# Which queue issues a perceiver kernel's last transfers: from SyncE's queue to ScalarE's, and the last two steps moved one by one

## The reference, cut to what matters

```
x = x + xattn(layernorm(x), ctx)      # 16 heads of 64: softmax(q k^T / 8) v, then @ w_out + b_out
x = x + attn(layernorm(x))            # three mixes of x with x shifted by one token,
                                      # k, v, r = their products; a decaying running sum over 512 tokens; @ Wo + bo
x = x + relu(layernorm(x) @ w1 + b1) @ w2 + b2
```

## Time and profile before

| | |
|---|---|
| three runs | 2408.26, 2411.14, 2415.79 us; median 2411.14 |
| the profiled execution | 2409.01 us, its span 2407.2 us |
| PE busy | 2300.2 us, 96% |
| DVE busy | 1833.4 us, 76% |
| ACT busy | 1545.8 us, 64% |
| POOL busy | 1606.9 us, 67% |
| DMA | 438.94 MB, mean 182 GB/s |

### The profile page before, as it was taken

The page is one execution under the profiler, slowest core; times in us unless marked ns, Lnnn a source line. Parts: engine busy times, 40 slices in busy tenths (PEclk is TensorE's granted clock), DMA queues, the critical chain, the costliest instruction groups (busy, mean ns, idle before and its releaser), DMA issues.

```text
span 2407.2 us, 44073 instructions
## 1 busy us (share of the span) xinstructions
PE 2300.2 (96%) x13696; PEld 2103.8 (87%) x13696; DVE 1833.4 (76%) x3669; ACT 1545.8 (64%) x2690; POOL 1606.9 (67%) x799
## 2 busy tenths in 40 slices
PE   4968999999999999999999999999999998879999
PEld 3648989999999999999999999999999998768788
DVE  7766777777777777777777777777777777679884
ACT  4655666667666676667666766767666765555444
POOL 2006878888888888888888888888888885421111
PEclk9989999999999999999999999999999999999999
DMA  5867888888888888888888888888888886786000
GB/s 155 240 200 165 195 193 195 197 198 206 200 200 199 201 198 199 198 201 200 200 200 200 201 200 199 199 199 201 198 199 199 198 196 160 171 209 173 14 10 27
DMA packets 384511, 438.94 MB, mean 182 GB/s; under 512 B 81600, under 2 KB 355392, under 8 KB 384448
## 3 DMA queue, kind: packets, MB, share of 16 engines
q1 hardware_dynamic: 384448, 438.14, 77.0%
HBM read 167.42 MB, written 52.43 MB: 91 GB/s over the span
## 4 chain that ended last, share of the span: by engine, by line
POOL 40%; issue 22%; PE 20%; DVE 4%; SPq 4%; ACT 1%; DMA 1%; POOLq 0%; ACTq 0%; DVEq 0%
POOL p_pt_lo L785 21%; POOL p_nat L812 6%; PE p_scores L1437 6%; POOL p_q_lo L797 5%; POOL p_ct_lo L793 4%; POOL p_ct_hi L804 4%; PE p_acc L1453 3%; SPq L640 3%; PE p_scores L1559 2%; PE p_cols L1501 2%; PE p_scores L1605 2%; PE p_cols L1592 2%; PE p_acc L1455 1%; PE p_scores L1517 1%; PE p_acc L1559 1%
## 5 line engine op out<-in xcount | busy, mean ns | idle before, releaser
L785 POOL TENSOR_TENSOR p_pt_lo<-p_landed,p_pt_hi 128x768 fp32r<-128x768 f32 x504 | 991.6, 1989 | 329.5 <-ACT p_pt_hi L927 329.5
L1453 PE MATMUL p_acc<-p_nat,p_pt_hi 128*128 128x384 f32 x3024 | 889.0, 361 | 16.3 <-POOL p_pt_lo L785 15.2
L1455 PE MATMUL p_acc<-p_nat,p_pt_lo 128*128 128x192 f32 x3024 | 759.3, 251 | 0.0
L1437 PE MATMUL p_scores<-p_ct_hi,p_q_hi 128*128 128x512 f32 (+2 forms) x2048 | 706.5, 348 | 25.6 <-DVE p_ct_hi L1377 13.8
L963 ACT ACTIVATE p_prob<-p_scores,p_negmax 128x800 f32<-128x800 f32 (+1 forms) x512 | 471.4, 926 | 398.7 <-DVE p_negmax L1189 398.5
L1437 PE MATMUL p_scores<-p_ct_hi,p_q_lo 128*128 128x512 f32 (+2 forms) x2048 | 705.8, 348 | 0.0
L1453 PEld LDWEIGHTS p_acc<-p_nat,p_pt_hi 128*128 128x128 f32 x3024 | 569.0, 188 | 23.9 <-issue 13.3
L1455 PEld LDWEIGHTS p_acc<-p_nat,p_pt_lo 128*128 128x128 f32 x3024 | 578.5, 191 | 0.0
L927 ACT ACTIVATE p_pt_hi<-p_landed 128x768 fp32r<-128x768 f32 x504 | 398.5, 838 | 163.4 <-PE p_acc L1457 125.7
L1437 PEld LDWEIGHTS p_scores<-p_ct_hi,p_q_hi 128*128 128x128 f32 x2048 | 390.6, 191 | 71.7 <-issue 14.2
L1197 DVE STREAM_TRANSPOSE turned<-p_prob 128x1536 f32<-128x1536 f32 x256 | 452.7, 1768 | 0.0
(11 more groups left out here) (228 smaller groups left out, 3130.0 us busy)
## 6 DMA issues: line engine op xcount, KB each, us to landing
p_landed<-turned SPq DMA_DIRECT2D x2048, 104.0 KB, 2.3
resid<-in_ctx SPq DMA_DIRECT2D x128, 288.0 KB, 4.9
o_scratch<-resid SPq DMA_DIRECT2D x256, 96.0 KB, 2.7
qk_scratch<-p_out_a SPq DMA_DIRECT2D x16, 1024.0 KB, 4.7
p_raw<-o_scratch SPq DMA_DIRECT2D x32, 512.0 KB, 4.9
p_stage<-qk_scratch SPq DMA_DIRECT2D x31, 512.0 KB, 3.9
p_stage<-qk_scratch SPq DMA_DIRECT2D x62, 256.0 KB, 4.4
p_stage<-in_ctxT SPq DMA_DIRECT2D x31, 401.0 KB, 4.7
```

What stands on the lines that cost most here:

```text
L785: nc.gpsimd.tensor_tensor(pt_lo[:, t0:t1, :, :], by_tile(slot, t0, t1), bits(pt_hi[:, t0:t1, :, :]), ALU.subtract).then_inc(pt_lo_done, 1)
L1437: last = nc.tensor.matmul(scores[:, S0 + lo:S0 + hi], w, x, start=m == 0, stop=m == len(terms) - 1)
L1453: nc.tensor.matmul(acc[k % 2][:, 0:2 * DC], pt_hi[:, t, :, :].rearrange("p i x -> p (i x)"), x[:, t, :], start=t == 0, stop=False, skip_gr ...
L1455: nc.tensor.matmul(acc[k % 2][:, 0:DC], pt_lo[:, t, :, :].rearrange("p i x -> p (i x)"), x[:, t, 0:DC], start=False, stop=False, skip_grou ...
```

## The change

Five edits, all at the end of the attention. The three transfers of the value weights, that of `w_out`, and the loads 0 to 10 leave SyncE's list and are issued by ScalarE, at places in its own list. The move of steps 254 and 255 is no longer one of 16 transfers for both: step 254 is moved by 16 transfers of half the size from SyncE, as soon as its transposes are done, and step 255 by eight from SyncE and eight from ScalarE, with semaphores of their own. On ScalarE `o_hi(0)` comes one step later, behind the `high` of u = 6. On ScalarE the `o_hi(2)` changes places with two `last_high`. The second half of `last_low(1)` goes from GpSimd to VectorE, and `out_weights_lo` there comes behind it. PE's list stays the same, but for the semaphore counts it waits on.

In the diff, after the two helpers, come SyncE's list (in the last batch and behind it), GpSimd's, ScalarE's (the last pass, then what follows it) and VectorE's.

```
+        def load_pair(eng, n):
+            c, j = divmod(n, HP)
+            src = by_pair(o_dram)[j, :, c * CB:(c + 1) * CB, :]
+            eng.dma_start(oa[n % RAW], src[0:P]).then_inc(o_in[n % RAW], 16)
+            for r in range(2):
+                eng.dma_start(ob[n % RAW][r * DCB:(r + 1) * DCB], src[P:DC, :, r * NQ:(r + 1) * NQ]).then_inc(o_in[n % RAW], 16)
+
+        def move_last(eng, j, parts):
+
+            slot = slice(2 + j, 3 + j)
+            for i in parts:
+                for g in range(G):
+                    dst = landed[g * R:(g + 1) * R, slot, i, :, :].rearrange("p s t x -> p s (t x)")
+                    eng.dma_start(dst, turned[i * R:(i + 1) * R, slot, g * GK:(g + 1) * GK]).then_inc(moved_last[j], 16)
...
-                    if ends:
-                        load_values()
...
-                    if ends:
-                        load(0)
...
-            load(1)
-            load(2)
-            move(NB * PPB - 1, 1, False)
-            load(3)
+            for j in range(2):
+                sp.wait_ge(pt_lo_done, (STEPS - LAG - 1 + j) * 2)
+                sp.wait_ge(turned_done, STEPS - 1 + j)
+                move_last(sp, j, range(G) if j == 0 else range(G // 2))
             store(NB - 1, 0)
             sp.wait_ge(wo_lo_done, 1)
             load_x(0)
-            load(4)
             load_x(1)
-            load(5)
-            load(6)
             store(NB - 1, 1)
...
-            load(7)
-            load(8)
...
-            for n in range(9, 17):
+            for n in range(11, 17):
...
-            last_low(0, halves); last_low(1, halves); last_low(2, halves[:1]); last_low(3, halves[:1])
+            last_low(0, halves); last_low(1, halves[:1]); last_low(2, halves[:1]); last_low(3, halves[:1])
...
+                    if ends and u == 5:
+                        load(0)
+                    if ends and u == 6:
+                        o_hi(0)
                     if ends and u == SB - 1:
+                        load(1)
+                        load(2)
                         last_high(0)
                     step(r, j, first)
+                    if ends and u == 0:
+                        load_values()
...
+                    if ends and u == 3:
+                        load_out_weights()
...
-                    if ends and u == 5:
-                        o_hi(0)
...
-            last_share(0); last_high(1); at(0); o_hi(1); o_hi(2); last_share(1); last_high(2); last_high(3); last_share(2); at(1); o_hi(3); at(2)
+            last_share(0); last_high(1); load(3); at(0); o_hi(1); last_move(); last_share(1); last_high(2); o_hi(2); load(4); last_high(3)
+            last_share(2); at(1); o_hi(3); load(5); at(2); last_share(3); o_hi(4); load(6); at(3); last_share(4); o_hi(5); load(7); at(4)
...
-            last_out(0); out_weights_lo(); at(0); o_lo(1); last_out(1); last_low(2); o_lo(2); last_low(3); last_out(2); at(1); o_lo(3); at(2)
+            last_out(0); last_low(1); at(0); out_weights_lo(); o_lo(1); last_out(1); last_low(2); o_lo(2); last_out(2); last_low(3); at(1); o_lo(3)
```

60 lines of the change are left out of this document (32 added, 28 removed).

## The result

The changed kernel takes 2397.84 us (median of 5 runs, 2396.03 to 2400.83), the kernel before 2411.14 beside it (2408.26 to 2415.79): ratio 0.9943, 95% interval 0.9928 to 0.9958. The forecast was 2400, in a range from 2394 to 2411. The profiled execution has a span of 2394.6 us, 12.6 less than that of before. A second set of the changed kernel (e12) stood 8.3 us under the kernel before beside it (2400.14 for 2408.40; ratio 0.9960, interval 0.9944 to 0.9976). The two intervals overlap, and the forecast gain of 11 lies between 13.3 and 8.3: the size of the gain is known no better than that.

A forecast was written before the change was run, and what follows sets the result against it. PE was taken to wait, through ScalarE, for transfers issued late in SyncE's one list. The gains, running to 11 us behind v(10), gave 2411.14 - 11 = 2400 us (profiled execution 2409.01 - 11 = 2398), range 2394 to 2411.

The forecast's parts named there:

- Part 1: Value weights and w_out issued from ScalarE, behind the exponentials of step 248: gain 0.7 us, w_out 0.
- Part 2: load(0) and the turn of step 250, high before o_hi(0): gain 4.5 us at the exponentials of 255, value weights included.
- Part 3: Moves of the last two steps: last_high(2) 7.2 us sooner, gain at v(2) 7.5 to 8 us.
- Its data has waited since 2063.5: At last_high(2): step 254's move landed at 2063.5, so ScalarE's own issues are now in its way.
- Part 5: Half of last_low(1) on VectorE: 1 us at v(1), gone again at product 254, so 0.
- Part 4: load(4) to load(10) from ScalarE: v(7) 12 to 14 us ahead, gain behind v(10) 11 us.
- The term taken off behind `v(7)`: At v(8) and v(9): 2 us lost because their loads share the DMA engines with last store, biases and square weights.
- The issue on ScalarE: Time per transfer issued on ScalarE: 0.58 us taken, SyncE's mean for a load; possible from next to nothing to 1.28.
- Rival A: ScalarE becomes the bound of the handover, from about 1.1 us per issue: 8 us slower, 2419; chance 0.08.
- Rival C: Issues nearly free on ScalarE beside its activations: gain 14 to 15 us, 2396; chance 0.15.
- D: No change: the later stretch is held by VectorE's own list; within 5 us, 2408; chance 0.10.
- B: Loads land late on full DMA engines and eat the late gain: 6 us left, 2405; chance 0.20.

The follow-up runs named there:

- e12: The changed kernel once more, unchanged, measured beside the kernel before: 2400.14 us, ratio 0.9960.
- e1 to e3: e1, e3 and, between them, the changed kernel with load(4) to load(10) back in SyncE's list: 2400.17 us, ratio 0.9951.
- e1: The changed kernel, but the last two steps moved together again by 16 transfers of SyncE: 2404.89 us, ratio 0.9972.
- e3: The changed kernel, but all 16 transfers of step 255's move issued by SyncE: 2400.24 us, ratio 0.9956.
- e4: The kernel before, with only o_hi(0) put behind the high of step 250 on ScalarE: 2404.85 us, ratio 0.9976.
- e6: The changed kernel with GpSimd's bias addition to x made to wait until VectorE is past o_lo(9): 2402.19 us, ratio 0.9963.
- e8: The changed kernel with each load split into six transfers of half the size instead of three: 2400.80 us, ratio 0.9961.

## Why the prediction was right, and where it wasn't

The time was right, and the three gains came where they were put. The sum of 11 us is partly luck: several of its terms were off, and in opposite directions.

**Part 1** held: ScalarE's wait of 0.78 us for the value weights is gone, and the exponentials of step 250 come 0.9 us sooner for 0.7.

**Part 2** held: forecast 4.5 us at the exponentials of 255, measured 3.3 in the changed kernel and 4.6 to 4.9 in e1 to e3, the remainder being the product of step 246 that ran slowly in the former (1.3 us). e4 shows that the order alone makes 5.0 us of time. PE's wait is 1.1 us for 6.46. One step of it failed: with "2.24 of landing" the move of steps 250 and 251 was not there. Beside `load(0)` its landing took 4.9 us, and the `high` of step 250 waited 3.41 us for it. That is the first sign of what Part 3 met.

**Part 3** had the gain and the wrong reason. `last_high(2)` was forecast 7.2 us sooner and came 8.4, `v(2)` 7.5 to 8 and came 6.4 (2077.50). The step "Its data has waited since 2063.5" failed: beside three loads a landing takes 5 to 8 us and not 2.24, and the data came at 2067.5, 0.4 us before ScalarE's queue was free. That ScalarE's own issues are in its way is true, but without them (e3) it starts only 0.9 us sooner, counted from step 253. The split itself is needed: without it (e1) some 5 to 7 us are lost. And what is missing at `v(2)` is due to neither. PE does product 254 without a wait; it had waited at `v(1)`, which is Part 5's matter.

**Part 4** was right up to `v(7)`: forecast 12 to 14 us, measured 13.1 (2099.14, less the 2.07). That is partly luck: `v(2)` was 1.4 us late, and the 2 us for ScalarE as the slower engine over six turns did not come, since it waited for PE in each of them. The term taken off behind `v(7)` was too small, 2 forecast and 3.3 measured (13.1 at `v(7)`, 9.8 at `at(10)`), and its reason was at most half of it. The whole loss stands at `v(8)` (9.7 at `at(8)`). In the first profile it is PE's wait of 3.19 us for `o_lo(8)`, slowed beside GpSimd's bias, and 1.3 us of lower clock behind it, and no landing. In the second (e12) a late `load(8)` adds 1.8 us to that wait. Loads 9 and 10 hold PE only when the bias is moved (`load(10)` 12.6 us in e6). VectorE's idle time had covered the collision before. I had counted GpSimd as spared and never asked what it runs beside once VectorE no longer waits.

**Part 5** was put at 0, and that failed. `out_weights_lo` and `o_lo(1)` came late behind the half of `last_low(1)`, and PE waited 2.05 us (1.08 in e12) and ran `v(1)` 1.4 us longer. The forecast counted 1 us at `v(1)`, "gone again at product 254, which waits for the move anyway". But product 254 didn't wait, so nothing of it was gone. (The diff also puts `last_low(3)` one place back on VectorE, which the list of edits leaves out.) No run puts the half of `last_low(1)` back on GpSimd, so what it costs in all is open.

**The issue on ScalarE**, 0.58 us taken: 0.33 to 0.80 each (0.55 on average) for the loads of the turns, 0.68 for `load(1)` and `load(2)`, 0.80 for the eight of step 255, both beside SyncE's. So the value was right for the first and up to 0.2 too low for the others. Rival A needed about 1.1, and two issuing queues did not double the price to 1.28. Its mechanism is real (two waits of "issue", e8).

**Sum**: 2409.01 - 11 = 2398 for the profiled execution, which took 2396.41. Of the 12.6 us in the profile 2.1 are of another place, so that 10.5 stand against the forecast's 11. Rival C (14) gave too much, D (3) too little. B's mechanism, the late landing, was there, but not where B put it: in the moves of steps 250 and 254, and at `v(8)` in one of the two profiles, beside GpSimd's bias.

In total: the order 5.0 us by the medians, the split of the last move some 5 to 7 where the rest is there, loads 4 to 10 3.6 in the profile and not to be told from zero in the times. e1, which has the loads but not the split, is no faster than e4: the parts don't add up in any order.

## What to carry to other kernels

Where transfers stand in one list with the waits of others, look for those whose data was ready, and change the order first: here one such exchange, of `high` and `o_hi(0)`, was worth 5 of the 8 to 13 us. When such a wait goes, ask of every engine what it will now run beside: the idle time of the waiting engine had covered a collision with GpSimd, and loads issued early were put among the small moves that the next step needs. Holds that lie side by side show little when one of them is taken away; here each edit alone gave 1.4 us or less at the tenth pair, and all of them 5.9. And a cost that one lets vanish in a later wait has to be counted when that wait is what the change removes. Before places of two profiles are compared, look for the last one that no edit can have touched: here 1.3 us stood there already.
